# Exponentials and value products of two attentions run four and seven beats ahead of their maxima, with rewritten joints to the feed-forward stages

## The chip, the core and the metric

The kernel runs on one core of a Trainium2 chip. The metric is the device time of one execution in microseconds (us); the time before is the median of three runs. The engines are TensorE (PE), VectorE (DVE), ScalarE (ACT), GpSimd (POOL) and SyncE (SP), which only issues DMAs here. Each engine executes its own instructions strictly in order and waits on semaphores.

## What is computed

For 16 sequences of 512 tokens and 128 features, in float32, four sublayers follow each other, each added to its input:

```python
x = x + attn_a(layernorm(x))   # 16 heads of 8, causal mask, three heads up-weight a token region
x = x + ffn(layernorm(x))      # silu(x w1) * (x w2), gelu(h1), gelu(h2), w3; hidden width 512
x = x + attn_b(layernorm(x))   # 16 heads of 8, rotary q and k, no mask
x = x + ffn(layernorm(x))      # the same weights
# attention: softmax(q k^T / sqrt(8)) v, heads concatenated, output projection
```

## The kernel before

**Stages.** The first attention ("causal") goes over all 16 sequences, then the first feed-forward stage (FFN) over all 16, then the second attention ("rotary"), then the second FFN. A sequence is called a batch below. A function `attention` makes the code of both attentions, `feed_forward` that of both FFN stages. At a joint, the end of one stage and the start of the next are written into each other by hand.

**An attention is a pipeline of steps, and a step is a row of beats.** A step has 20 beats (causal) or 32 (rotary). In step n five batches are in work: x of batch n+1 is normalised, transposed and projected to q; k and v of batch n are made; the row maxima of batch n-1 are found; scores, exponentials and value products of batch n-2 are made; the result of batch n-3 is normalised and that of batch n-4 projected. One beat of the maxima is some matmuls into `ps_max` (L1003, L1020) and one reduction of VectorE (`negmax`, L854 or L850). One beat of the scores, for a pair of heads and 128 keys each, is matmuls into two of the three banks of `ps_score` (L985), two exponentials of ScalarE into `prob` (L971), and, causal, a mask on GpSimd that waits for both (L708). Value products (L1043) gather in `ps_out` over a group of beats; four times in a batch ScalarE copies `ps_out` to `o_raw` (`group_out`, L934), at score beats 8, 13, 18 and 23 (causal) or 12, 20, 28 and 36 (rotary). A score beat of 20 (32) and over lies in the next step.

**The order** is set by two tables, `CAUSAL_AT` and `ROTARY_AT`, that give each piece of work its beat in each engine's loop, and by the order in which a step's beat is written. For every engine the program is one list made by the loops `tensor`, `vector`, `scalar`, `pool_step`. On PE a beat is the scores, the maxima, the value products, then other work (`order`: S, M, W, X).

**The maxima go into the scores** as two more rows of the stationary q ("aug"). GpSimd splits the negated maxima in two bf16 parts (`P_nm0`, `P_nm1`, for the first and second half of the heads), PE transposes them (`nm0`, `nm1`), ScalarE copies them to `nm_rows` (`A_nm0`, `A_nm1`, L908), and SP sends them into `stack_q` by DMA (L548). The scores of the first half of the heads wait for the first of these, the scores of the second half (score beat 10 or 16) for the second.

**The queue of SP** in step n is, in this order: load of `stack_q` of batch n (L592), which waits until the parts stored last have landed; load of x of batch n+3 (causal, L282); second aug of batch n-2; `den` and four `o_num` out of `o_raw` of batch n-3 (L555, L558); store of the parts of k of batch n (L580, six DMAs); store of the reciprocals (L563); load of `stack_k` (L592); four `o_rden` (L570); first aug of batch n-1; store of the parts of q of batch n+1 (L580, six DMAs). Steps 8 and 9 of the causal attention have one more small DMA each, for a flag that says whether FFN weights have a low part (`FLAG_STEP`, L629).

**`o_raw` is one buffer.** The first copy of a batch waits until all four `o_num` of the batch ahead of it have landed:

```python
def group_out(act, b, G):
    act.wait_ge(s["pv"], count(BLOCKS, b, BLOCKS // GROUPS * (G + 1)))
    wait(act, s["den"], count(16, b))
    wait(act, s["o_in"], count(64, b))
    act.activation(m["o_raw"][:, G], m["ps_out"][:], ACT.Copy).then_inc(s["o_raw"], 1)
```

**q and k** come to DRAM in three bf16 parts, which GpSimd makes in two pieces: `high` (L671, L673; rotary, also the sum L668, after VectorE's `turned`, L831) at beats `P_q1`, `P_k1`, and `middle_low` (L678, L680) at `P_q2`, `P_k2`. In the causal attention these stand between masks: at beat 16 `high` of q, then the mask of beat 16, at beat 17 `middle_low` of q. The normalisation (L313 to L322) is at beat 7, ahead of the mask of that beat, and `middle_low` of k at beat 8.

**At a joint** PE finishes the step without maxima (B + 1), reads the flag, branches (`tensor_both`, two versions of the FFN code), and then mixes the last value products with the first FFN products. In the last batch of the first FFN the first maxima of the rotary attention are mixed in.

## Time and profile before

| | us |
|---|---|
| median of 3 runs | 2166.25 |
| lowest and highest | 2159.3, 2166.3 |
| the profiled execution | 2165.54 |
| its span | 2163.4 |
| PE busy | 1941.8 (90%) |
| VectorE busy | 1724.5 (80%) |
| ScalarE busy | 1475.7 (68%) |
| GpSimd busy | 1092.3 (50%) |

The stages lie one after another in the span: causal attention to about 613 us, FFN to about 955, rotary attention to about 1780, FFN to the end. A share over the whole span says little for one of them; the sections below read single steps (a causal one is 406.90 to 440.10, a rotary one 1394.30 to 1440.60). "Idle before" in a row is time in which the engine did nothing ahead of the instruction, with the instruction or DMA that ended it.

### The profile page before, as it was taken

The page shows a single profiled execution, that of the slowest core. Times are in us where ns is not written, and L with a number is a line of the kernel's source. Part 1 is how long each engine was busy: PE and PEld are TensorE (multiplying, and loading weights), DVE is VectorE, ACT ScalarE, POOL GpSimd, SP SyncE. Part 2 cuts the span into 40 slices and gives each one's busy share as a digit, 9 for nine tenths or more (in the row PEclk, how much of TensorE's full clock was granted, in tenths as well). Part 3 has the DMA queues.
Part 4 walks back from the last instruction along what each step waited for, and adds up shares of the span by engine and source line. Part 5 has one row for each costly group of instructions (what it writes and reads, how often), then busy time and mean ns, then how long its engine had stood idle before and what let it go on. Part 6 is the DMA issues. An engine that isn't in the chain of part 4 may idle for free.

```text
span 2163.4 us, 43052 instructions
## 1 busy us (share of the span) xinstructions
PE 1941.8 (90%) x16196; PEld 987.2 (46%) x16196; DVE 1724.5 (80%) x2353; ACT 1475.7 (68%) x2633; POOL 1092.3 (50%) x1550
## 2 busy tenths in 40 slices
PE   3888987998869999986799999999999978999998
PEld 1333443433337777764222222222222226777776
DVE  4888886887758888865899898999989926888883
ACT  1477776776856666642488888888888874666665
POOL 5777776776535555555333333434333013555554
PEclk6799998999989999998799999999999988999999
DMA  7456655655200000003444443344445000000000
GB/s 174 94 116 131 118 110 113 133 114 114 39 18 29 1 1 1 1 1 71 77 81 90 87 91 71 71 91 90 97 77 100 18 13 12 15 11 15 10 15 15
DMA packets 106357, 136.71 MB, mean 63 GB/s; under 512 B 21153, under 2 KB 90018, under 8 KB 100002
## 3 DMA queue, kind: packets, MB, share of 16 engines
q1 hardware_dynamic: 106146, 133.89, 30.8%
q8 instruction: 133, 2.18, 0.4%
q14 instruction: 78, 0.64, 0.1%
HBM read 67.78 MB, written 55.58 MB: 57 GB/s over the span
## 4 chain that ended last, share of the span: by engine, by line
PE 52%; POOL 11%; SPq 10%; DMA 10%; issue 8%; DVE 6%; ACT 4%; POOLq 0%; ACTq 0%; DVEq 0%
PE ps_score L1416 21%; PE ps_out L1043 8%; PE ps_max L1416 6%; PE ps_score L985 5%; DMA o_num<-o_raw 4%; PE ps_max L1003 4%; DVE negmax L854 4%; SPq L580 3%; DMA d_stack<-parts 3%; PE ps_out L1416 2%; ACT prob L971 2%; PE ps_max L1084 2%; SPq L558 2%; POOL xhat L322 2%; DMA stack_q<-nm_rows 2%
## 5 line engine op out<-in xcount | busy, mean ns | idle before, releaser
L971 ACT ACTIVATE prob<-ps_score 128x512 f32<-128x512 f32 x1664 | 898.9, 597 | 191.7 <-PE ps_score L985 173.6
L854 DVE TENSOR_REDUCE negmax<-ps_max 128x2 f32<-128x1024 f32 (+1 forms) x896 | 907.5, 1064 | 144.0 <-PE ps_max L1020 88.6
L1043 PE MATMUL ps_out<-prob,v_aug 128*9 128x256 f32 (+2 forms) x6656 | 514.4, 389 | 24.7 <-ACT o_raw L934 22.0
L1416 PE MATMUL ps_score<-h,w_hi 128*128 128x512 f32 x2048 | 506.3, 401 | 0.7 <-ACT h2f L1333 0.4
L1416 PEld LDWEIGHTS ps_score<-h,w_hi 128*128 128x128 f32 x2048 | 387.0, 191 | 96.4 <-issue 3.7
L985 PE MATMUL ps_score<-stack_q,stack_k 50*128 50x512 bf16 (+3 forms) x2048 | 358.1, 349 | 59.6 <-ACT prob L971 46.4
L1003 PE MATMUL ps_max<-stack_k,stack_q 48*128 48x512 bf16 (+3 forms) x2048 | 343.5, 353 | 59.8 <-DVE negmax L854 28.7
L1195 POOL TENSOR_TENSOR h<-h3f,h 128x512 fp32r<-128x512 f32 x128 | 191.5, 1506 | 159.9 <-ACT h L1339 159.9
L708 POOL TENSOR_SCALAR_AFFINE_SELECT prob<-prob 128x256 f32<-128x256 f32 (+1 forms) x448 | 188.3, 440 | 148.7 <-ACT prob L971 148.1
L985 PEld LDWEIGHTS ps_score<-stack_q,stack_k 50*128 50x128 bf16 x2048 | 105.5, 94 | 312.6 <-ACT prob L971 241.1
L1043 PEld LDWEIGHTS ps_out<-prob,v_aug 128*9 128x9 f32 x6656 | 106.2, 89 | 300.7 <-ACT prob L971 147.2
L1195 POOL TENSOR_TENSOR h<-h2f,h 128x512 fp32r<-128x512 f32 x128 | 173.4, 1356 | 63.3 <-ACT h L1339 63.3
L1003 PEld LDWEIGHTS ps_max<-stack_k,stack_q 48*128 48x128 bf16 x2048 | 87.5, 95 | 218.4 <-DVE negmax L854 99.5
L1333 ACT ACTIVATE h3f<-ps_score,s_col 128x512 f32<-128x512 f32 x128 | 87.6, 684 | 144.1 <-PE ps_score L1416 133.1
L668 POOL TENSOR_TENSOR qf<-qf,turned 128x512 f32<-128x512 f32 x32 | 41.2, 1286 | 262.3 <-DVE turned L831 262.3
L1416 PE MATMUL ps_max<-ffn_xT,w_hi 128*128 128x512 f32 x512 | 147.4, 422 | 20.4 <-DVE ffn_xT L1257 10.7
L1250 DVE CAST h<-h1f 128x512 fp32r<-128x512 f32 x128 | 130.5, 1020 | 38.5 <-PE ps_score L1416 34.6
L1333 ACT ACTIVATE h2f<-ps_score,s_col 128x512 f32<-128x512 f32 x128 | 88.1, 688 | 88.9 <-PE ps_score L1416 86.2
L1237 DVE SCALAR_TENSOR_TENSOR ut<-tanh,ps_max 128x512 f32<-128x512 f32 x128 | 86.9, 679 | 59.4 <-ACT tanh L1345 56.6
L332 DVE TENSOR_SCALAR xhat<-x,mv,rstd 128x128 f32<-128x128 f32 x128 | 94.5, 797 | 44.1 <-POOL rstd L304 44.1
L1252 DVE TENSOR_TENSOR h<-h1f,h 128x512 fp32r<-128x512 f32 x128 | 118.8, 928 | 4.4
L1416 PEld LDWEIGHTS ps_max<-ffn_xT,w_hi 128*128 128x128 f32 x512 | 95.6, 197 | 54.3 <-DVE ffn_xT L1257 23.7
(107 smaller groups left out, 2105.2 us busy)
## 6 DMA issues: line engine op xcount, KB each, us to landing
d_stack<-parts SPq DMA_DIRECT2D x128, 192.0 KB, 2.8
stack_q<-d_stack SPq DMA_DIRECT2D x64, 384.0 KB, 5.6
stack_k<-d_stack SPq DMA_DIRECT2D x64, 384.0 KB, 6.1
d_stack<-parts SPq DMA_DIRECT2D x128, 128.0 KB, 2.8
d_stack<-parts SPq DMA_DIRECT2D x128, 64.0 KB, 2.5
o_num<-o_raw SPq DMA_DIRECT2D x128, 64.0 KB
o_rden<-d_rden SPq DMA_DIRECT2D x128, 64.0 KB
x<-in_x SPq DMA_DIRECT2D x16, 256.0 KB, 6.9
```

The costliest lines, as they stand in the source:

```text
L332: last = dve.tensor_scalar(m["xhat"][:, t, :], m["x"][:, b % B, t, :], m["mv"][:, t, 0:1], m["rstd"][:, t:t + 1], ALU.subtract, ALU.mult)
L708: last = pool.affine_select(out=tri, in_=tri, compare_op=ALU.is_ge, fill=0.0, base=0, pattern=[[0, tri.shape[1]], [1, P]], channel_multipl ...
L854: last = dve.tensor_reduce(m["negmax"][:, t, :, p], banks[:, :, at:at + w], AX.X, ALU.max, negate=True)
L971: act.activation(prob(b, i)[:, o], act_bank("score", 2 * i + o), ACT.Exp).then_inc(s["prob"], 1)
L985: mm = pe.matmul(act_bank("score", 2 * i + o)[:, at:at + w], m["stack_k"][c][rows, p, P * j:P * (j + 1)], m["stack_q"][c][rows, p, S - w:S ...
L1003: last = pe.matmul(to[:, o, at:at + w], m["stack_q"][c][rows, p, P * t:P * (t + 1)], m["stack_k"][c][rows, p, 0:w], start=(piece == 0), st ...
L1043: last = pe.matmul(m["ps_out"][32 * g:32 * g + HD + 1, out:out + w], m["v_aug"][b % VALUES][:, j, 4 * G + g, :], prob(b, beat)[:, g % 2, l ...
L1195: pool.tensor_tensor(h[k][:, 1, f], hf[k][:, f % 2], h[k][:, 0, f], ALU.subtract).then_inc(s[f"h{k}"], 1)
L1250: dve.tensor_copy(h[1][:, 0, f], h1f[:, f % 2]).then_inc(s["h1_hi"], 1)
L1252: dve.tensor_tensor(h[1][:, 1, f], h1f[:, f % 2], h[1][:, 0, f], ALU.subtract).then_inc(s["h1"], 1)
L1333: act.activation(hf[k][:, f % 2], m["ps_hid"][:, f % 2], ACT.Gelu, scale=m["s_col"][:, k, f:f + 1]).then_inc(s[f"h{k}f"], 1)
L1416: mm = pe.matmul(to, w[:, cols], moving(part), start=begin and i == 0, stop=last and i == len(pairs) - 1)
```

## The change

**Shift.** Both tables get a number `ahead`: 4 beats (causal) and 7 (rotary). In beat i of step n, PE makes the scores and value products, ScalarE the exponentials and the copies to `o_raw`, and GpSimd the masks, of position i + ahead; positions past the end belong to the next step. Maxima, q, k, v, normalisation, aug copies and the whole queue of SP stay at their beats, but for the entries of the tables that the diff shows. So the first copy to `o_raw` of batch n-2 stands at beat 4 of step n (causal; it was 8) and at beat 5 (rotary; it was 12), and the first scores of batch n-1 at beat 16 (of 20) and beat 25 (of 32) of step n, not at beat 0 of step n+1.

**Tables.** Causal: `nm0` and `A_nm0` one beat earlier; the second piece of low weights at beat 8 of step 1, not 13. Rotary: `nm0` 23 to 18, `P_nm0` 19 to 16, `A_nm0` 24 to 19, `P_nm1` 8 to 0, `P_norm` 15 to 17, `xT`, `q` and their followers one beat later.

**Flag.** Its two DMAs go from steps 8 and 9 to 10 and 11, the reduction that reads it from step 10 to 13.

**Joints.** PE takes the branch four beats ahead of the end of the scores, and the first FFN gate follows at the end of the scores. In an FFN's first batch ScalarE makes the high part of h1 and GpSimd the low part; VectorE made both. At the end of the first FFN fewer of the first rotary maxima stand between its last products (2, 2 and 2 beats before, 3, 2 and 2 now), and VectorE, not GpSimd, makes the parts of the first k.

```diff
-W_LOW_AT = ((0, 19), (1, 13), (1, 5), (1, 5), (1, 5))
+W_LOW_AT = ((0, 19), (1, 8), (1, 5), (1, 5), (1, 5))
...
-CAUSAL_AT = {... "nm0": 13, ... "A_nm0": 14, ... "order": "MSWX"}
-ROTARY_AT = {... "xT": 19, "nm0": 23, "q": 23, ... "P_nm1": 8, "P_norm": 15,
-             "P_q1": 24, ... "P_nm0": 19, ... "D_q": 24, ... "A_nm0": 24, "A_xT": 20, "order": "SMWX"}
+CAUSAL_AT = {... "nm0": 12, ... "A_nm0": 13, ... "order": "MSWX", "ahead": 4}
+ROTARY_AT = {... "xT": 20, "nm0": 18, "q": 24, ... "P_nm1": 0, "P_norm": 17,
+             "P_q1": 25, ... "P_nm0": 16, ... "D_q": 25, ... "A_nm0": 19, "A_xT": 21, "order": "SMWX", "ahead": 7}
...
+    def ahead(n, i):
+        return divmod(BEATS * n + i + AHEAD, BEATS)
...
-        if causal and n == FLAG_STEP:
+        if causal and n == FLAG_STEP + 2:
...
-            if causal and on(n, 2):
-                mask(pool, n - 2, i)
+            step, at = ahead(n, i)
+            if causal and on(step, 2):
+                mask(pool, step - 2, at)
...
-            for lag, G in plan.out_due(i):
-                if on(n, lag):
-                    group_out(act, n - lag, G)
+            step, k = ahead(n, i)
+            for lag, G in plan.out_due(k):
+                if on(step, lag):
+                    group_out(act, step - lag, G)
...
+            step, k = ahead(n, i)
             for part in AT["order"]:
-                if part == "S" and on(n, 2):
-                    scores(pe, n, i)
+                if part == "S" and on(step, 2):
+                    scores(pe, n, step - 2, k)
...
-        gates(first, 0)
-        gates(first, 1)
-        before.tensor(pe, B + 2)
-        gates(first, 2)
-        gates(first, 3)
-        pe.wait_ge(over["prob"], count(2 * before.plan.beats, B))
-        transposes(pe, first + 1)
+        gates(first, 0)
+        before.tensor(pe, B + 1, scored)
+        gates(first, 1)
+        pe.wait_ge(over["prob"], count(2 * before.plan.beats, B))
+        transposes(pe, first + 1)
+        gates(first, 2)
+        gates(first, 3)
```

**ScalarE, causal, a steady step.** `nm_rows` ahead of `prob x2` or `x4` and `o_raw` is the second aug copy. Before:

```order
105 L908 ACTIVATE nm_rows<-ps_score 16x512
106 L971 ACTIVATE prob<-ps_score 128x512 x2
107 L934 ACTIVATE o_raw<-ps_out 128x512
108 L971 ACTIVATE prob<-ps_score 128x512 x6
109 L925 ACTIVATE v_aug<-ps_max 128x64x8
110 L971 ACTIVATE prob<-ps_score 128x512 x4
111 L934 ACTIVATE o_raw<-ps_out 128x512
```

Now:

```order
107 L933 ACTIVATE nm_rows<-ps_score 16x512
108 L996 ACTIVATE prob<-ps_score 128x512 x4
109 L959 ACTIVATE o_raw<-ps_out 128x512
110 L996 ACTIVATE prob<-ps_score 128x512 x4
111 L950 ACTIVATE v_aug<-ps_max 128x64x8
```

The `o_raw` of row 107 before is the batch's last copy; the first copy of the next batch is row 111, twelve exponentials and a value copy behind the aug copy. Now the first copy is row 109, four exponentials behind the aug copy.

**ScalarE, rotary, a steady step**, from the second aug copy to the batch's first copy to `o_raw`. Before:

```order
640 L908 ACTIVATE nm_rows<-ps_score 16x512
641 L934 ACTIVATE o_raw<-ps_out 128x512
642 L971 ACTIVATE prob<-ps_score 128x512 x16
643 L934 ACTIVATE o_raw<-ps_out 128x512
644 L971 ACTIVATE prob<-ps_score 128x512 x8
```

Now:

```order
634 L933 ACTIVATE nm_rows<-ps_score 16x512
635 L996 ACTIVATE prob<-ps_score 128x512 x2
636 L959 ACTIVATE o_raw<-ps_out 128x512
637 L996 ACTIVATE prob<-ps_score 128x512 x16
638 L959 ACTIVATE o_raw<-ps_out 128x512
```

Sixteen exponentials stood between the two; now two do.

**GpSimd, causal, around the parts of q** (beats 15 to 17), before:

```order
223 L708 AFFINE_SELECT prob<-prob 128x4x128
224 L708 AFFINE_SELECT prob<-prob 128x2x128
225 L671 CAST parts<-qf 128x512
226 L673 TENSOR_TENSOR rest<-qf,parts 128x512
227 L708 AFFINE_SELECT prob<-prob 128x2x128
228 L678 CAST parts<-rest 128x512
229 L680 TENSOR_TENSOR parts<-rest,parts 128x512
```

Now:

```order
218 L714 AFFINE_SELECT prob<-prob 128x2x128 x6
219 L714 AFFINE_SELECT prob<-prob 128x4x128
220 L677 CAST parts<-qf 128x512
221 L679 TENSOR_TENSOR rest<-qf,parts 128x512
222 L714 AFFINE_SELECT prob<-prob 128x2x128
223 L684 CAST parts<-rest 128x512
224 L686 TENSOR_TENSOR parts<-rest,parts 128x512
```

The mask ahead of the parts of q was that of score beat 15 and is that of score beat 19, the last of a batch; the one between their halves was that of score beat 16 and is the first of the next batch.

## Rows read from the trace of the kernel before

**Rows 1.** The page: busy time, share and instructions of each engine.

```profile
PE 1941.8 (90%) x16196; PEld 987.2 (46%) x16196; DVE 1724.5 (80%) x2353; ACT 1475.7 (68%) x2633; POOL 1092.3 (50%) x1550
```

**Rows 2.** By stretch: length, busy PE, PEld, DVE, ACT, POOL; PEclk, DMA, GB/s.

```profile
406.90:440.10 33.20, 30.55 (x400) 13.06 (x394) 27.88 (x42) 25.15 (x49) 25.45 (x52) 0.95 0.61 121
...
1394.30:1440.60 46.30, 43.21 (x422) 12.32 (x421) 41.80 (x47) 38.46 (x72) 16.29 (x24) 1.00 0.42 83
```

**Rows 3.** Waits of the whole span: who waited for whom, us, times, longest.

```profile
ACT o_raw L934 <- DMA o_num<-o_raw: 44.6, 22, 11.4
```

**Rows 4.** Timeline of ScalarE, one causal step: start, us, operation, count, idle before.

```profile
433.52 0.60 ACT L934 ACTIVATE o_raw<-ps_out 128x512 f32<-128x512 f32 x1 [2.65 <-DMA o_num<-o_raw]
...
437.37 1.08 ACT L971 ACTIVATE prob<-ps_score 128x512 f32<-128x512 f32 x2 [0.55 <-PE ps_score L985]
...
444.42 3.44 ACT L971 ACTIVATE prob<-ps_score 128x512 f32<-128x512 f32 x6 [0.44 <-PE ps_score L985]
...
449.64 2.14 ACT L971 ACTIVATE prob<-ps_score 128x512 f32<-128x512 f32 x4
```

**Rows 5.** Timeline of GpSimd, the same step.

```profile
430.01 0.24 POOL L313 TENSOR_SCALAR var<-mv 128x4 f32<-128x4 f32 x1
...
433.77 0.78 POOL L708 TENSOR_SCALAR_AFFINE_SELECT prob<-prob 128x256 f32<-128x256 f32 x2
...
435.20 1.16 POOL L680 TENSOR_TENSOR parts<-rest,parts 128x512 bf16<-128x512 f32 x1
...
447.13 0.61 POOL L671 CAST parts<-qf 128x512 bf16<-128x512 f32 x1
```

**Rows 6.** Timeline of SP's queue, the same step and the next.

```profile
443.88 2.78 SPq L570 DMA_DIRECT2D o_rden<-d_rden  x4
446.70 1.39 SPq L548 DMA_DIRECT2D stack_q<-nm_rows  x2
451.18 3.90 SPq L580 DMA_DIRECT2D d_stack<-parts  x6
...
458.54 1.37 SPq L548 DMA_DIRECT2D stack_q<-nm_rows  x2
```

**Rows 7.** Chain of work that ended last: start, us, what; landings of DMAs.

```profile
381.45 3.78 DMA stack_q<-nm_rows
...
454.46 2.42 DMA d_stack<-parts
...
462.86 4.25 DMA o_num<-o_raw
```

**Rows 8.** Timeline of VectorE: reciprocals, causal steps 3 and 15, rotary 3 and 15.

```profile
130.45 0.54 DVE L862 RECIPROCAL rden<-den 128x64 f32<-128x64 f32 x1
...
541.19 0.54 DVE L862 RECIPROCAL rden<-den 128x64 f32<-128x64 f32 x1
...
1120.07 0.54 DVE L862 RECIPROCAL rden<-den 128x64 f32<-128x64 f32 x1
...
1669.26 0.54 DVE L862 RECIPROCAL rden<-den 128x64 f32<-128x64 f32 x1
```

**Rows 9.** Timelines of one rotary step: VectorE, then ScalarE.

```profile
1414.38 0.75 DVE L831 SCALAR_TENSOR_TENSOR turned<-ps_max,bias_col,rope 128x512 f32<-128x512 f32 x1 [0.22 <-PE ps_max L1084]
...
1425.47 3.31 ACT L971 ACTIVATE prob<-ps_score 128x512 f32<-128x512 f32 x6 [0.36 <-PE ps_score L985]
1429.84 5.53 ACT L971 ACTIVATE prob<-ps_score 128x512 f32<-128x512 f32 x10 [1.06 <-PE ps_score L985]
1436.56 0.60 ACT L934 ACTIVATE o_raw<-ps_out 128x512 f32<-128x512 f32 x1 [1.19 <-DMA o_num<-o_raw]
```

**Rows 10.** Chain of work, around the flag's DMA in step 8.

```profile
311.19 11.17 DMA d_stack<-parts
```

**Rows 11.** Timelines of PE at the first joint and the rotary attention's last step.

```profile
616.83 3.75 PE L1416 MATMUL ps_max<-ffn_xT,w_hi 128*128 128x512 f32 x8 [3.98 <-issue]
...
1742.30 0.59 PE L1054 MATMUL ps_score<-ident_b,nm_parts 128*16 128x128 bf16 x4 [4.24 <-POOL nm_parts L653]
```

More of the change, by code:

```diff
@@ L440, in attention @@
     for i in range(BEATS):
-        act_turns += [("score", 2, 2 * i + o) for o in range(2)]
+        step, at = ahead(0, i)
+        act_turns += [("score", 2 - step, 2 * at + o) for o in range(2)]
         dve_turns += [("max", 1, i)]
@@ L900, in vector @@
             gate_scales(dve)
-        if causal and hi == BEATS and n == FLAG_STEP + 2:
+        if causal and hi == BEATS and n == FLAG_STEP + 5:
             flag_of_weights(dve)
@@ L946, in scalar @@
             weights_hi(act)
-        if causal and n == 2 and lo == 0:
-            act.wait_ge(s["w_lo"], len(W_PIECES))
         for i in range(lo, hi):
+            if causal and ahead(n, i) == (2, 0):
+                act.wait_ge(s["w_lo"], len(W_PIECES))
             if i == AT["A_nm1"] and on(n, 2):
@@ L1204, in pool_layer @@
         left["weighted"](pool, B - 2)
+        for f in range(FT):
+            pool.wait_ge(s["h1_hi"], count(FT, first, f + 1))
+            pool.tensor_tensor(h[1][:, 1, f], h1f[:, f % 2], h[1][:, 0, f], ALU.subtract).then_inc(s["h1"], 1)
+        left["weighted"](pool, B - 1)
         for r in range(B):
@@ L1222, in pool_layer @@
                 fill["high"](pool, 0, "q", 0)
-                low(pool, b, 3, range(0, 2))
                 fill["middle_low"](pool, 0, 0)
-                low(pool, b, 3, range(2, 4))
-                fill["high"](pool, 0, "k", 1)
-                fill["middle_low"](pool, 0, 1)
+                low(pool, b, 3, range(FT))
             if r == B - 1:
@@ L1277, in vector_layer @@
         norm_apply(dve, m, s, first + 1)
-        for r in range(-1, B - 1):
+        gated(dve, first, 0)
+        gated(dve, first, 1)
+        for f in (2, 3):
+            dve.wait_ge(s["h1"], count(FT, first, f - 1))
+            gated(dve, first, f)
+            if f == 2:
+                left["invert"](dve, B - 1)
+        xT_low(dve, first + 1)
+        left["residual"](dve, B - 2)
+        for r in range(B - 1):
             b = first + r
+            fill = after.parts if after is not None and r == B - 2 else None
             gated(dve, b + 1, 0)
             gated(dve, b + 1, 1)
-            if after is not None and r == B - 2:
-                after.parts["project"](dve, 0, "q", 0)
-                after.parts["turn"](dve, 0, "q", 0)
-            if r == -1:
-                dve.wait_ge(before.s["pv"], count(before.plan.blocks, B))
-            if 0 <= r < B - 2:
+            if r < B - 2:
                 normed(b + 2)
+            if fill:
+                fill["project"](dve, 0, "q", 0)
+                fill["turn"](dve, 0, "q", 0)
             split(dve, b + 1, 0)
+            if fill:
+                fill["project"](dve, 0, "k", 1)
             split(dve, b + 1, 1)
-            if r == -1:
-                left["invert"](dve, B - 1)
-                left["residual"](dve, B - 2)
             if r == 0:
                 left["residual"](dve, B - 1)
-            if r > 0:
+            else:
                 add_y(dve, b - 1)
@@ L1299, in vector_layer @@
             split(dve, b + 1, 2)
-            if after is not None and r == B - 2:
-                after.parts["project"](dve, 0, "k", 1)
-                after.parts["turn"](dve, 0, "k", 1)
+            if fill:
+                fill["turn"](dve, 0, "k", 1)
+                fill["parts_on_vector"](dve, 0, "k", 1)
             gated(dve, b + 1, 3)
@@ L1308, in vector_layer @@
                 after.parts["statistics"](dve, 0)
-            if after is not None and r == B - 2:
-                after.parts["whole_bias"](dve, m["ps_misc"][:, 0:D])
-                after.parts["statistics"](dve, 1)
+            if fill:
+                fill["whole_bias"](dve, m["ps_misc"][:, 0:D])
+                fill["statistics"](dve, 1)
         add_y(dve, first + B - 2)
@@ L1360, in scalar_layer @@
         xT_high(act, first)
-        before.scalar(act, B + 1, 12)
+        scored = before.plan.beats - before.plan.at["ahead"]
+        before.scalar(act, B + 1, 12, scored)
         gate(act, first, 0)
+        before.scalar(act, B + 1, scored)
         gate(act, first, 1)
-        before.scalar(act, B + 2)
-        for r in range(-1, B):
+        high(act, first, 0)
+        high(act, first, 1)
+        gate(act, first, 2)
+        high(act, first, 2)
+        gate(act, first, 3)
+        xT_high(act, first + 1)
+        high(act, first, 3)
+        for r in range(B):
             b = first + r
@@ L1435, in layer @@
                         mm.then_inc(s[f"l{k}_ps"], 1)
-                if between is not None and i == 1:
-                    between()
         def gates(n, f):
@@ L1463, in tensor_layer @@
             layer(b, 2, (0,))
+            if r == 0:
+                gates(b + 1, 0)
+                gates(b + 1, 1)
             if fill and r == B - 2:
@@ L1539, in tensor_both @@
         transposes(pe, first)
-        before.tensor(pe, B + 1, 10)
+        before.tensor(pe, B + 1, 10, before.plan.beats - before.plan.at["ahead"] - 4)
         pe.wait_ge(s["halved"], 5)
```

116 lines of the change are left out of this document (65 added, 51 removed).

## The prediction, made blind

> **What bounds the kernel now.** The busy shares come first, and they mislead: PE is 90% busy and VectorE 80% [rows 1], so a schedule that packs beats more tightly looks like the thing to want. The stretches by step say more. A causal step takes 33.2 us with 30.55 of PE and 25.15 of ScalarE, a rotary step 46.3 with 43.2 of PE and 41.8 of VectorE [rows 2]: close to the engines' work, but not at it. What ends last in a step stands in the waits. The batch's first copy to `o_raw` waits for the `o_num` DMAs of the batch ahead, 22 times and 44.6 us in all [rows 3]. In the causal step read here it waited 2.65 us [rows 4], in the rotary one 1.19 [rows 9]. So in both attentions the copy is where a loop through ScalarE, GpSimd, SP's queue and two DMAs closes, and it has no slack left.
>
> The causal loop, from the copy at 433.52 to the next at 467.2: ScalarE runs score beats 8 to 15 until about 446.7 (four of six exponentials of the row that starts at 444.42) [rows 4]; GpSimd masks and starts the parts of q at 447.13 [rows 5]; SP stores them from 451.18 [rows 6]; they land at 456.88 (454.46 + 2.42) [rows 7]; SP loads `stack_q`, sends the second aug at 458.54 [rows 6], then `den` and `o_num`; the last `o_num` is issued at 462.86 and lands at 467.11 [rows 7]. That is 13.2 us on ScalarE, 0.4 for mask and start, 20.0 from the parts to the landing: 33.6. The twelve steps from the reciprocal at 130.45 to that at 541.19 [rows 8] took 34.2 each, or 33.4 without ten us lost near the flag (below).
>
> **The shift, causal.** The exponentials and copies move four beats ahead; SP's queue and the parts of q do not. The copy now stands at beat 4 and waits for the same DMAs, still issued behind the parts of q of beat 17. ScalarE has beats 4 to 15, score beats 8 to 19, between the copy and the mask ahead of the parts. Score beats 16 to 19 end at 451.8 (449.64 + 2.14) [rows 4], 5.1 us behind beat 15. So this loop alone gives 13.2 + 5.1 + 0.4 + 20.0 = 38.7.
>
> A second wait enters it. The mask between the halves of the parts of q is now the first of the next batch, whose scores need the first aug at beat 16. That aug is late in SP's queue. Counted from the copy (0): score beat 10 ends at 4.9 (437.37 + 1.08 - 433.52) [rows 4]; one mask 0.4; the normalisation 3.8 (430.01 to the mask at 433.77); two masks 0.8; the second half of the parts of k 1.9 (masks' end near 434.5 to 436.36) [rows 5]: 11.8. SP then stores k, 3.9 like q; landing 2.4 from the last issue: 17.5. Load of `stack_k` 0.8, `o_rden` 2.8, aug 1.4 [rows 6]: last issue at 21.8. It lands 3.8 to 3.9 later [rows 7]: 25.7, where ScalarE could have had beat 16 at 18.3. Scores and two exponentials 1.4, mask 0.4, second half of q 1.9: 29.4. From the store of q to the landing of `o_num` is 467.11 - 451.18 = 15.9. The period is **45.3 us** and not 33.4: +11.9. Over twelve steps, with the flag's ten us kept in either, that is +143. The steps of the last two batches have no q to store, but keep the wait from second aug to `o_num` (from 458.54 to 467.11, 8.6 us, against four exponentials, 2.2) and a shorter one at beat 16: about 7 + 7 + 4.5 + 7 less 5 of waits that were there, +20. At the start, -5 for four beats that are overlapped, +11 for the same two waits: +6. Causal sum **+169**.
>
> **The shift, rotary.** No masks here, and the first aug has ten beats from the reciprocal (beat 15) to beat 25, 14 us at 1.43 a beat. Behind the reciprocal come its store with a landing (3.3, estimated from the 0.6 and 2.4 of other stores), `o_rden` 2.8, the aug 0.7 to its last issue and 3.8 to land [rows 6, 7]: 10.6. I give it nothing. The loop runs from the copy to `turned` of beat 28, then parts, store, load, second aug, `o_num`, copy. From the end of `turned` at 1415.13 to the idle's end at 1436.5 is 21.4 [rows 9], none of which moves. The copy goes from beat 12 to beat 5; in between ScalarE now has 9.9 us (1425.47 to 1435.37) [rows 9]. The twelve steps from 1120.07 to 1669.26 [rows 8] took 45.8 each, so the loop becomes 45.8 + 9.9 = 55.7 at most; PE and VectorE may lose some gaps, of which they have 3 to 4.5 in a step [rows 2]: I take **55**, +9.2, or +110 over twelve. A check that does without q: the second aug copy stands two exponentials (1.1 us) ahead of the copy to `o_raw`, and aug, `den`, `o_num` and landing take 8.6 (458.54 to 467.11) [rows 6, 7], so ScalarE stands for 7.5 a step whatever else happens, and 45.8 - 1.2 + 7.5 is 52. The last two steps have this wait alone, +16. At the start +8 for the first such wait and -6 for seven overlapped beats: +2. Rotary sum **+128**.
>
> **The gains.** A beat of scores alone is 1.1 us (two exponentials) [rows 4] and one of maxima alone I estimate at 1.2, both together 33.4/20 = 1.67 or 45.8/32 = 1.43; four and seven fewer of each alone are worth about 3 and 6, counted above. `P_nm1` at beat 0 puts the split of the last maxima ahead of the FFN's normalisation on GpSimd: PE's wait of 4.24 us goes [rows 11], with some slow matmuls behind it: -5.5. The branch ahead of the last four beats of scores: the 3.98 us of issue at the joint [rows 11] can lie behind queued exponentials, and the mixed order saves some more. I take -8 at each joint (bounds 0 and -12), -16. High parts on ScalarE for one batch, fewer maxima between the last FFN products, the earlier second piece of low weights: each touches a single batch, 0 within 3 us either way. Sum of gains **-21.5**.
>
> **The flag.** In step 8 the store of q landed 11.17 us after its last issue instead of 2.4 [rows 10], with the flag's DMA issued right behind it. It is the only landing of that length in the chain, and the only store with that DMA behind it; the pair is kept two steps later, so I take 0. If the delay was its step's, -9.
>
> **Sum.** 2165.5 (the profiled execution, 0.7 below the median) + 169 + 128 - 21.5 = 2441; I say **2440 us**, 12.6% slower. About 0.5%, 11 us, is what a measurement here tells from no change.
>
> **Rivals.**
> 1. *The copy's wait alone.* If in the causal attention the first aug is in time (parts of k earlier on GpSimd than I count, or a quicker queue), its loop is 38.7: 12 x 6.6 and some 10 at the ends less, **2350**. For it: the queue has gaps that I fill. Against: the sum of issues alone, from the parts of k to the aug, is 3.9 + 0.8 + 2.8 + 1.4 us with two landings, and the reciprocal at beat 12 gates it too. Chance 0.2.
> 2. *The work packs around the wait.* The floor is PE's work plus a stand of 7 us: causal about 36, rotary about 51, so 12 x 2.6 + 12 x 5.2 + 44 (the ends, as above) - 21.5, **2280**. PE would have to run nearly without gaps outside the wait. Chance 0.06.
> 3. *Faster.* The waits cost nothing, because `o_num` lands before ScalarE gets to the copy. The price is then -3 - 6 - 21.5: **2135**. It decides at the point where the second aug and `o_num` take less than the two to four exponentials between: 8.6 us against 1.1 and 2.2. The 2.65 and 1.19 us of idle at today's places speak against it. Chance 0.03.
> 4. *The clock.* After today's wait PE runs slowly for a while: the causal step has a mean clock of 0.95, the rotary 1.00 [rows 2]. Two long stands a step (causal) and one (rotary) would leave more of the work at 1.2 GHz: 0.05 of 33 us is 1.7 us a time, over 24 steps some +40, **2480**. Chance 0.1. The Trainium skill states this in "TensorE: Matmul & The Clock Gate", Part 1: a PE that idles long enough is gated to half rate and speeds up only once busy again. It speaks against the change, which lengthens idling; today's rotary wait of 1.19 us with a clock of 1.00 shows the other side of it. By that rule the sum would be this rival's, by the rotary row my forecast's.
> My forecast, 2400 to 2470, has 0.6; 0.01 is left for within 0.5% of before.
>
> **How the numbers follow.** The range goes from rival 1's 2350 to rival 4's 2480; rivals 2 and 3, the 0.01 and the far side of either end are left out, 0.1 and some 0.08. Faster by over 0.5% 0.03, within 0.5% 0.01, slower 0.96.
>
> **What would show it.** The wait of `o_raw` on `o_num` in some 26 places, 5 to 10 us each, in place of 44.6 us in all. Reciprocals 45 us apart (causal) and 55 (rotary). In the causal attention a wait of the first scores of a batch on `stack_q<-nm_rows`, 5 to 8 us; if it is under 1 us, rival 1. The 4.24 us wait gone. FFN steps unchanged near 21.7. A store of q that lands ten us late near the flag's new step, or not. Wrong in kind would be a wait at the copy below 3 us in the steady steps.

## The result

The changed kernel took **2512.3 us** (median of four runs, 2510.9 to 2515.9) against 2165.0 before (2159.3 to 2166.3), a ratio of 1.161 (95% interval 1.159 to 1.164): 16% slower. The forecast was 2440, range 2350 to 2480. Direction and mechanism came as told. The size did not: 72 us are missing, and the time lies 32 above the range. The profiled execution took 2515.9 us, with a span of 2514.2 and a mean granted clock of 0.886 (before: 2163.4 and 0.950).

The page of the changed kernel has the same 16196 matmuls as [rows 1], but they are busy 74 us longer. Its PEclk line gives TensorE's granted clock in 40 slices, in tenths of full speed:

```profile
PE 2015.9 (80%) x16196; PEld 997.6 (40%) x16196; DVE 1725.4 (69%) x2342; ACT 1480.1 (59%) x2641; POOL 1099.9 (44%) x1553
...
PEclk6778788878888899999698888899898889999999
```

The waits (us in all, times, longest). The first answers to [rows 3]; the other two, weight loads and matmuls of the same scores, overlap:

```profile
ACT o_raw L959 <- DMA o_num<-o_raw: 238.8, 30, 14.6
...
PEld ps_score L1010 <- DMA stack_q<-nm_rows: 112.5, 18, 10.7
PE ps_score L1010 <- DMA stack_q<-nm_rows: 108.9, 18, 9.1
```

The reciprocals of causal steps 3 and 15 and rotary steps 3 and 15, as in [rows 8]:

```profile
148.25 0.54 DVE L887 RECIPROCAL rden<-den 128x64 f32<-128x64 f32 x1
...
739.34 0.54 DVE L887 RECIPROCAL rden<-den 128x64 f32<-128x64 f32 x1
...
1338.83 0.54 DVE L887 RECIPROCAL rden<-den 128x64 f32<-128x64 f32 x1
...
2024.79 0.54 DVE L887 RECIPROCAL rden<-den 128x64 f32<-128x64 f32 x1
```

A causal step takes 49.3 us instead of 34.2, a rotary one 57.2 instead of 45.8. Over twelve steps each that is +180 and +137, together 317 of the 347.

**One causal step**, from the first copy to `o_raw` of one batch to that of the next. ScalarE (start, us, operation, idle before):

```profile
577.67 0.60 ACT L959 ACTIVATE o_raw<-ps_out 128x512 f32<-128x512 f32 x1 [6.08 <-DMA o_num<-o_raw]
...
582.43 0.60 ACT L950 ACTIVATE v_aug<-ps_max 128x512 f32<-128x512 f32 x1 [2.04 <-PE ps_max L1112]
...
606.82 1.09 ACT L996 ACTIVATE prob<-ps_score 128x512 f32<-128x512 f32 x2 [7.78 <-PE ps_score L1010]
...
625.92 0.60 ACT L959 ACTIVATE o_raw<-ps_out 128x512 f32<-128x512 f32 x1 [6.04 <-DMA o_num<-o_raw]
```

SP's queue in the same step, which stands as in [rows 6]:

```profile
591.23 3.89 SPq L586 DMA_DIRECT2D d_stack<-parts  x6
...
597.46 0.79 SPq L598 DMA_DIRECT2D stack_k<-d_stack  x2
598.29 2.78 SPq L576 DMA_DIRECT2D o_rden<-d_rden  x4
601.11 1.39 SPq L554 DMA_DIRECT2D stack_q<-nm_rows  x2
610.21 3.91 SPq L586 DMA_DIRECT2D d_stack<-parts  x6
...
617.32 1.37 SPq L554 DMA_DIRECT2D stack_q<-nm_rows  x2
...
619.45 3.20 SPq L564 DMA_DIRECT2D o_num<-o_raw  x4
```

And the landings, from the chain of work that ended last (start, us):

```profile
509.55 10.22 DMA d_stack<-parts
...
594.52 2.88 DMA d_stack<-parts
...
601.84 4.24 DMA stack_q<-nm_rows
...
621.65 4.17 DMA o_num<-o_raw
```

Read them in turn. Parts of k are stored from 591.23. Their landing lets `stack_k` be loaded, then come `o_rden` and the first aug, whose last issue at 601.84 lands at 606.08. Only then do TensorE's scores and ScalarE's exponential at 606.82 go on, after a stand of 7.78 us. The parts of q, held up behind that score beat's mask on GpSimd, are stored from 610.21, and behind them stand the load, the second aug and `o_num`, which lands at 625.82. The copy at 625.92 waited 6.04 us for it. Both waits that the forecast named are there, and both are in one loop of 48.3 us (the first row of this list, 509.55, belongs to the flag, below).

**TensorE's rate behind a stand** is what the sum did not price. By stretch of one rotary step (length, busy time of PE, PEld, DVE, ACT, POOL, then the clock): the stand for the copy, then the seven us behind it.

```profile
1773.00:1782.00 9.00, 0.59 (x5) 0.09 (x4) 1.97 (x2) 0.48 (x2) 0.00 (x0) 0.62 0.66 122
1782.00:1789.00 7.00, 6.41 (x34) 1.15 (x34) 2.39 (x3) 3.39 (x7) 0.55 (x1) 0.51 0.00 0
```

A clock of 0.51 is the lower of the two levels, 1.2 GHz instead of 2.4. The products of this stretch show it in their length, 2.08 us for a pair of the same line that takes 1.12 at 1770.79, ahead of the stand:

```profile
1785.51 2.08 PE L1109 MATMUL ps_max<-xT,weights 128*128 128x512 f32 x2
```

The clock fell in this way in every one of the twelve rotary steps; its mean over them is 0.90.

### The profile page after: what moved, and what is told of

It is laid out like the page before. It is cut to its first block, busy times and chain, and to the rows that moved or that the text cites. A ratio compares the mean times of both kernels' runs of the same rounds, so it can differ in the third digit from the quotient of the medians.

```text
span 2514.2 us, 43055 instructions
## 1 busy us (share of the span) xinstructions
PE 2015.9 (80%) x16196; PEld 997.6 (40%) x16196; DVE 1725.4 (69%) x2342; ACT 1480.1 (59%) x2641; POOL 1099.9 (44%) x1553
## 4 chain that ended last, share of the span: by engine, by line
PE 52%; SPq 12%; DMA 12%; issue 8%; POOL 8%; ACT 5%; DVE 3%; POOLq 0%; ACTq 0%; DVEq 0%
PE ps_score L1460 18%; PE ps_out L1068 10%; PE ps_score L1010 7%; DMA o_num<-o_raw 5%; PE ps_max L1460 5%; PE ps_max L1028 4%; SPq L586 4%; ACT prob L996 4%; DMA d_stack<-parts 3%; DMA stack_q<-nm_rows 3%; SPq L564 2%; PE ps_max L1109 2%; PE ps_out L1460 2%; SPq L554 2%; SPq L576 2%
## 5 line engine op out<-in xcount | busy, mean ns | idle before, releaser
L1068 PE MATMUL ps_out<-prob,v_aug 128*9 128x256 f32 (+2 forms) x6656 | 549.0, 412 | 158.7 <-ACT o_raw L959 152.8
L1010 PE MATMUL ps_score<-stack_q,stack_k 50*128 50x512 bf16 (+3 forms) x2048 | 380.0, 367 | 234.6 <-ACT prob L996 118.6
L1460 PEld LDWEIGHTS ps_score<-h,w_hi 128*128 128x128 f32 x2048 | 381.9, 188 | 104.6 <-POOL h L1233 10.8
L1028 PE MATMUL ps_max<-stack_k,stack_q 48*128 48x512 bf16 (+3 forms) x2048 | 356.5, 364 | 45.1 <-DVE negmax L879 24.1
L674 POOL TENSOR_TENSOR qf<-qf,turned 128x512 f32<-128x512 f32 x31 | 39.5, 1274 | 469.3 <-DVE turned L856 469.3
L959 ACT ACTIVATE o_raw<-ps_out 128x512 f32<-128x512 f32 x128 | 77.1, 602 | 243.3 <-DMA o_num<-o_raw 238.8
L875 DVE TENSOR_REDUCE negmax<-ps_max 128x4 f32<-128x1024 f32 x64 | 77.4, 1209 | 119.4 <-PE ps_max L1045 118.7
L1275 DVE CAST h<-h1f 128x512 fp32r<-128x512 f32 x120 | 124.4, 1037 | 34.8 <-PE ps_score L1460 33.7
```

Of the source, the lines that this page charges most:

```text
L1010: mm = pe.matmul(act_bank("score", 2 * i + o)[:, at:at + w], m["stack_k"][c][rows, p, P * j:P * (j + 1)], m["stack_q"][c][rows, p, S - w:S ...
L1028: last = pe.matmul(to[:, o, at:at + w], m["stack_q"][c][rows, p, P * t:P * (t + 1)], m["stack_k"][c][rows, p, 0:w], start=(piece == 0), st ...
L1068: last = pe.matmul(m["ps_out"][32 * g:32 * g + HD + 1, out:out + w], m["v_aug"][b % VALUES][:, j, 4 * G + g, :], prob(b, beat)[:, g % 2, l ...
L1275: dve.tensor_copy(h[1][:, 0, f], h1f[:, f % 2]).then_inc(s["h1_hi"], 1)
L1460: mm = pe.matmul(to, w[:, cols], moving(part), start=begin and i == 0, stop=last and i == len(pairs) - 1)
```

## The experiments

"Spacing" is always the mean distance of twelve reciprocals, taken as in [rows 8], causal and rotary. All kernels are edits of the changed one unless it says otherwise.

| kernel | us | causal | rotary | wait of `o_raw`, all |
|---|---|---|---|---|
| before | 2165.0 | 34.2 | 45.8 | 44.6 |
| changed | 2512.3 | 49.3 | 57.2 | 238.8 |
| without shift | 2134.5 | 34.0 | 45.8 | 50.3 |
| causal shift alone | 2341.0 | 48.6 | 45.7 | 110.6 |
| rotary shift alone | 2300.3 | 34.4 | 56.9 | 158.4 |
| half the shift | 2305.2 | 40.7 | 51.1 | 77.2 |
| numerators first | 2421.8 | 46.5 | 53.2 | 141.5 |
| first aug first | 2418.5 | 42.6 | 57.3 | 267.4 |
| both | 2305.5 | 38.5 | 53.0 | 146.5 |
| both, second aug too | 2292.7 | 37.9 | 53.0 | 144.4 |
| no shift, numerators first | 2106.6 | 33.3 | 44.7 | 0.8 |
| no shift, both | 2104.8 | 33.2 | 44.7 | 3.5 |
| before, numerators first | 2152.1 | 34.4 | 45.2 | 3.2 |

### The parts of the change

**No shift.** The tables, the flag's place and the joints stay new; both shifts are zero.

```diff
-CAUSAL_AT = {... "order": "MSWX", "ahead": 4}
-ROTARY_AT = {... "order": "SMWX", "ahead": 7}
+CAUSAL_AT = {... "order": "MSWX", "ahead": 0}
+ROTARY_AT = {... "order": "SMWX", "ahead": 0}
...
+        if not before.plan.at["ahead"]:
+            before.tensor(pe, B + 2)
```

ScalarE's list gets the same two lines.

> The changed kernel with both shifts set to 0 (scores, exponentials, copies and masks back at their beats); the changed joints, the other table entries and the later flag stay. Theory (the shift alone costs, through the copy to o_raw that waits for the o_num DMAs): within -30 to 0 us of the kernel before, 2135 to 2165, causal reciprocals 33 to 34 us apart, rotary ones 45 to 46. Rival (the other table entries or the joints carry part of the loss): above 2200. If the flag's small DMA is the cause of the ten us in step 8, they appear in step 10 or 11 instead.

Measured: 2134.5 us, a ratio of 0.988 (0.985 to 0.991) to before, and the spacing is that of before. So all else in the change is worth -27 us (forecast -21.5), and the shift alone costs 378. The -27 is against the 2161.7 that the kernel before took beside this one; against the 2165.0 of the table it is -30.5.

The flag's write (L635) stands right behind the store of q here too, but the ten us did not come with it. The store's last issue is at 381.45 and `stack_q`, which waits for its landing, is loaded from 383.57, so it landed within 2.1 us:

```profile
377.54 4.52 SPq L586 DMA_DIRECT2D d_stack<-parts  x6
382.10 0.58 SPq L635 DMA_DIRECT2D d_flags<-flags  x1
383.57 3.60 SPq L598 DMA_DIRECT2D stack_q<-d_stack  x2
```

**Each shift alone**, one of the two numbers set to zero (and the joint's lines as above).

> The changed kernel with the rotary shift set to 0, the causal shift of 4 kept. Theory: the causal steps stay 49 apart and the rotary ones go back to 46, so 2512 less 12 x 11.3 and the two waits at the end of the rotary attention (16) = 2360, within 15. Rival (the two shifts share one cost, such as one of the joints): the saving is under 80 us.

> The changed kernel with the causal shift set to 0, the rotary shift of 7 kept. Theory: the causal steps go back to 33.5, the rotary ones stay at 57: 2512 less 12 x 15.1 (49.3 - 34.2) and some 25 at the ends = 2305, within 15. e2 and e3 together minus e1 should give the changed kernel within 10 us.

Measured: 2341.0 (causal) and 2300.3 (rotary), 4 us under the band of the first and inside that of the second. Against the kernel without shift the causal one costs 207 us, the rotary one 166. Their sum on 2134.5 is 2507, 5 below the changed kernel, so the two hardly act on each other.

**Half the shift**, two beats and three.

```diff
-CAUSAL_AT = {... "order": "MSWX", "ahead": 4}
-ROTARY_AT = {... "order": "SMWX", "ahead": 7}
+CAUSAL_AT = {... "order": "MSWX", "ahead": 2}
+ROTARY_AT = {... "order": "SMWX", "ahead": 3}
```

> The changed kernel with half the shift: two beats in the causal attention, three in the rotary one (the joints then finish what is left over). Theory: each beat of shift puts its own length between the copy to o_raw and the transfers that it waits for, so the loop grows in proportion: rotary about 50.5 us (45.8 unshifted, 57.2 with seven), causal about 42 (34.0 and 48.6 to 49.3), some 2310 us in all, 2270 to 2340. Rival: the schedule has slack for a few beats and the waits set in only beyond them: 2200 us or less.

Measured: 2305.2 us. The rotary step grows by 5.3 us for three beats and 11.4 for seven, 1.8 and 1.6 a beat; the causal one by 6.7 for two and 15.3 for four, 3.4 and 3.8 a beat. There is no sign of a threshold: the price starts with the first beats, as it must in a loop that had no slack.

### The order in SP's queue

**Numerators first.** `den` and `o_num` stand ahead of the load of `stack_q` and the second aug. They need the last copy to `o_raw` and, because `o_num` is one buffer too, the product `oT` of the batch ahead (GpSimd, beat 1 causal, 0 rotary), but not the parts of q.

```diff
+        if on(n, 3):
+            numerators(sp, n - 3)
         if on(n, 0):
             load(sp, n, "stack_q", "stored_q", 0)
         if causal and on(n, -X_AHEAD):
             load_x(sp, m, a, n + X_AHEAD)
         if on(n, 2):
             aug(sp, 1, n - 2)
-        if on(n, 3):
-            numerators(sp, n - 3)
```

> The changed kernel with one move in SP's queue: den and o_num stand ahead of the load of stack_q and of the second aug. Theory (the copy to o_raw waits for o_num behind the parts of q and the second aug): o_num then waits for the store of q and for oT of GpSimd's beat 1 (causal) or 0 (rotary); it lands about 1.5 us earlier in the causal step and 4 in the rotary one, so 2512 - 12 x 1.3 - 12 x 4 = 2450, within 20, and the copy's wait of 8.5 us in a rotary step falls to 4 or 5. Rival (the wait at the copy is not what sets the period, but PE work at the half clock or the first aug): less than 15 us.

Measured: 2421.8 us, 91 less, more than the band allowed. The copy's wait falls from 238.8 to 141.5 us, as the theory has it, while the wait for the first aug stays:

```profile
ACT o_raw L959 <- DMA o_num<-o_raw: 141.5, 30, 5.9
...
PEld ps_score L1010 <- DMA stack_q<-nm_rows: 106.1, 27, 10.5
```

The numerators are then held up in part by `oT` (SP waits 52.3 us for it, in 16 places).

**First aug first.**

```diff
+        if on(n, 1):
+            aug(sp, 0, n - 1)
         if on(n, 3):
             store_reciprocals(sp, n - 3)
         if on(n, 0):
             load(sp, n, "stack_k", "stored_k", 1)
         if on(n, 3):
             spread_reciprocals(sp, n - 3)
-        if on(n, 1):
-            aug(sp, 0, n - 1)
```

> The changed kernel with one issue moved in SP's row: the first augmented row of batch n-1 stands ahead of the store of the reciprocals and the load of parts of k, instead of behind them. Theory: at the causal part's block boundary TensorE's next score tile (beat 16) waits for that transfer; issued at the end of the beat before it lands some 6 us earlier, so this wait all but ends, while the wait of the first o_raw copy, which comes from the second half of the row, stays. The causal step falls from 49.3 us to about 43 us, the rotary one stays at 57.2: about 2440 us. Rival: the wait for the first row only covers time that the copy wait would take anyway (the loop closes over the second half); then under 20 us is won.

Measured: 2418.5 us, 94 less, 22 below the 2440 expected. The causal step is 42.6, the rotary one unchanged at 57.3. The wait for the first aug is gone and the copy's has grown, the other way round than in the run before:

```profile
ACT o_raw L959 <- DMA o_num<-o_raw: 267.4, 30, 14.4
...
PEld ps_score L1010 <- DMA stack_q<-nm_rows: 5.7, 2, 4.5
```

The two runs tell the two waits apart. The second wait is real, and it is worth 6.7 us a causal step. The forecast had 6.6 for it, the distance from rival 1's 38.7 to 45.3.

**Both, and the second aug ahead of the load of `stack_q` as well.**

```diff
+        if on(n, 3):
+            numerators(sp, n - 3)
+        if on(n, 2):
+            aug(sp, 1, n - 2)
         if on(n, 0):
             load(sp, n, "stack_q", "stored_q", 0)
```

> The changed kernel, fully shifted, with both moves in SP's row: the numerators ahead of the load of stack_q and the second augmented row, and the first augmented row ahead of the reciprocals' store. Theory: they cut two different waits, won about 90 and 94 us apart, so together 2330 us (2305 to 2350), still far above the unshifted kernel, since the parts of q stay unshifted ahead of both. Rival: one loop closes over both, and the second move gives nothing more: 2400 us or above.

> As the last one, with the second augmented row moved ahead of the load of stack_q too: now nothing stands ahead of numerators and augmented rows in SP's row but the store of the parts of q. Theory: the second row lands about 1 us earlier, in both attentions, 10 to 30 us below the last kernel. Rival: the load of stack_q is then late for the maxima and their first beats: no gain or a loss.

Measured: 2305.5 with both moves, 207 less than the changed kernel, where the two single gains add up to 184; 25 us below the point expected, at the band's edge. 2292.7 with the third move, 13 less, 7 of them in the causal steps. With nothing but the store of the parts of q ahead of them in the queue, the numerators still land late, 144.4 us in 30 waits, and the kernel is 158 us slower than the one without shift. No order of these transfers that I tried saves the shift while the parts of q stay at their beat. The numerators ahead of the store of q, or the parts of q moved with the exponentials, were not tried.

### The missing 72 us: the clock behind the stands

The waits were as foreseen, so the suspect was the stretch at half clock. To price it, TensorE gets work in its stand that enters nothing of the result: matmuls into the next maxima bank, which is written anew before it is read.

```diff
+    def keep_busy(pe, n, i, products):
+        dve_banks_free(pe, n, "max", i)
+        for _ in range(products):
+            pe.matmul(dve_banks("max", i)[:, 0, 0:S], ...)
...
                     if part == "W" and on(step, lag):
+                        if rotary and block == BLOCKS // GROUPS and 3 <= n < B:
+                            keep_busy(pe, n, i + 1, ...)
                         weigh(pe, step - lag, block)
```

**First try**: 32 bf16 matmuls of 512 columns with the operands of the maxima. They have 48 rows (`48*128` in the trace), not the 50 that the expectation of the second try names.

> The changed kernel with work added that computes nothing of the result: in each rotary step 3 to 15, where TensorE stands for the first o_raw copy, 32 matmuls of 512 columns run into a max bank that is overwritten later. Theory: what the forecast's sum lacked is the stretch at half clock behind this stand; with the engine busy in it the clock stays up, the rotary step falls from 57.2 us to 54.5 to 55, and the kernel to about 2480 us although it does some 90 us more of TensorE work. Rival: the long step is the transfers' chain alone and the half clock lies beside it: under 8 us of change, or slower by what the added work hangs over.

Measured: 2517.0 us, rotary spacing 57.5: nothing gained. But nothing was tested either, since the clock fell during the added work. The same columns as above, first 4.6 us of it, then the rest and what follows:

```profile
1713.20:1717.80 4.60, 4.57 (x22) 2.01 (x23) 1.11 (x1) 0.00 (x0) 0.00 (x0) 1.00 0.89 153
1717.80:1728.20 10.40, 10.30 (x38) 2.38 (x36) 1.89 (x2) 2.73 (x6) 0.00 (x0) 0.51 0.16 25
```

**Second try**: 14 float32 products over all 128 rows.

> The changed kernel with work added that computes nothing of the result, in the stand of each rotary step 3 to 15: 14 float32 matmuls of 512 columns over all 128 rows of the array, instead of 32 bfloat16 ones over 50 rows, which did not keep the clock up. Theory: what counts for the clock is how much of the array works, then the half clock behind the stand goes and the rotary step falls from 57.2 us to about 55, some 30 us in all (2480). Rival: no such work changes the clock in this stretch: within 8 us of 2512.

Measured: 2520.1 us, rotary spacing 57.9. The clock stayed up this time, in the stand and behind it:

```profile
1661.30:1673.60 12.30, 12.24 (x32) 5.27 (x36) 1.13 (x1) 1.57 (x3) 0.00 (x0) 1.00 0.44 81
1673.60:1680.00 6.40, 6.40 (x63) 1.51 (x62) 4.85 (x5) 4.29 (x8) 2.65 (x3) 1.00 0.00 0
```

By its number this is the rival's (within 8 us of 2512), but not by its reason, since the clock did change. The work is 12.3 us long and the stand about 9, so some 3 us hang over, as much as the clock can give back. The third try tests that.

**Third try**: 10 such products, 8.9 us.

> As the last one with added float32 work over 128 rows, but 10 products (20 passes, about 8.8 us) instead of 14 (12.3 us), so that the work ends with the stand of 9 us. Nothing of it enters the result. Theory: the half clock behind the stand costs about 2.3 us a step, which the forecast lacked: rotary step 57.2 to 54.5 to 55.2, kernel 2480 to 2490 us. Rival: the stretch at half clock lies beside a longer chain and costs nothing: rotary step 57 and more, 2510 or above.

Measured: **2480.0 us**, 32 less, with more work done. The stand and the stretch behind it, then the reciprocals of rotary steps 3 and 15:

```profile
1699.90:1708.80 8.90, 8.85 (x24) 3.76 (x28) 1.13 (x1) 0.69 (x2) 0.00 (x0) 1.00 0.61 110
1708.80:1716.00 7.20, 7.20 (x73) 1.73 (x74) 5.66 (x6) 5.97 (x12) 3.46 (x4) 1.00 0.01 3
```

```profile
1339.85 0.54 DVE L887 RECIPROCAL rden<-den 128x64 f32<-128x64 f32 x1
...
1994.20 0.54 DVE L887 RECIPROCAL rden<-den 128x64 f32<-128x64 f32 x1
```

The seven us behind the stand now hold 73 matmuls, not 34. The step is 54.5 us, where the forecast had 55 and the changed kernel has 57.2. So the half clock costs 2.6 us a rotary step, 32 over twelve, the whole gain of this run. The granted clock of the twelve steps is 1.00, where it was 0.90, and the copy's wait is the same (234.1 us in all): the chain of transfers did not change.

**The same in both attentions**, with 7 products ahead of the scores of beat 0 and 5 ahead of those of beat 9 in the causal one.

```diff
+                if causal and part == "S" and k in (0, 9) and 3 <= n < B:
+                    keep_busy(pe, n, i + 1, {0: 7, 9: 5}[k])
```

> The same, and in the causal steps 3 to 15 too: 7 products (6.1 us) ahead of the scores of beat 0, where TensorE stands for the first augmented row, and 5 (4.4 us) ahead of those of beat 9, where it stands behind the o_raw copy. Nothing of it enters the result. Theory: the causal step falls from 49.3 to 46 or 47 us (the forecast had 45.3), kernel 2435 to 2460 us. Rival: in the causal loop the half clock costs nothing, or the work hangs over: 2480 or above.

Measured: 2463.2 us, 17 less again and 3 above the band. The causal step is 47.3, and the granted clock of twelve causal steps is 0.97, where it was 0.82. The same causal code stood between 48.6 and 49.3 in the six profiles that have it, so keeping the clock gives back 1.3 to 2.0 us a step there. Where the added work hangs over a stand, this is less than what the clock costs.

**Rows or type?** 40 bf16 matmuls over 128 rows (8.5 us) in the rotary stand.

> The changed kernel with 40 bfloat16 matmuls of 512 columns over 128 rows (8.5 us) in the rotary stand; nothing of it enters the result. Theory: the rows of the array that work are what counts; the clock stays up as with float32, and the rotary step is 54.5 to 55.5. Rival: it is the type (float32 in two passes); then the clock falls as with the 50-row bfloat16 work, step 57.

Measured: 2490.5 us (two runs), rotary spacing 55.3, and the clock of the stand is 1.00:

```profile
1699.70:1708.30 8.60, 8.58 (x39) 3.72 (x38) 0.86 (x1) 0.00 (x0) 0.00 (x0) 1.00 0.73 128
```

So bf16 as such isn't what let the clock fall in the first try. The two bf16 kinds differ in their rows (48 and 128), and in their number (32 and 40) and length (6.8 us at full clock and 8.6).

### A version that beats both

The copy's wait is in the kernel before too [rows 3], and it needs no shift to be removed.

**No shift, numerators first**: the edits of those two kernels together.

> Both attentions unshifted (as in the run without shifts) and the new joints kept, with the transfers that put the numerators back (the reciprocal row and the product to o_num) issued ahead of the load of stack_q and the second augmented row in SP's queue. Theory: of the 1.9 us mean wait of the o_raw copy per step (50.3 us in 27) most ends, and TensorE's half clock behind it with it: causal step about 31.5 us instead of 34.0, rotary 44.8 instead of 45.8, so about 2095 us, 2070 to 2125. Rival: the load of stack_q, now behind the numerators, comes late for the next score tile and gives it back: within 15 us of 2134.

Measured: **2106.6 us**, 0.975 of before (0.971 to 0.979), 28 less than without the move; 12 above the point expected, inside its range; the causal step is 33.3 where 31.5 was expected. The wait at the copy is gone, while the weight loads of the scores now wait 25.0 us for aug rows, in 23 places (4.8 in 6 without the move):

```profile
ACT o_raw L959 <- DMA o_num<-o_raw: 0.8, 2, 0.6
```

The twelve rotary steps (1132.80 to 1667.60) have 519.67 of 534.80 us of PE busy, 97%, at a clock of 1.00, so little idle time is left in them.

**The first aug first as well.**

> As the unshifted kernel with the numerators issued first, and the first augmented row of batch n-1 issued first as well. Theory: in the unshifted loop TensorE waits little for that row, so the move gives 0 to 15 us over the kernel with the numerators first alone: 2080 to 2100 us. Rival: the reciprocals' store and the load of parts of k, now behind it, come later and lengthen the step: 2110 us or more.

Measured: 2104.8 us, 0.973 (0.969 to 0.978): 5 above the band expected and no different from the last within what can be measured. Without the shift the first aug has time.

**Before, numerators first**, the move alone in the kernel before.

> The kernel before with one move: the numerators ahead of the load of stack_q and the second augmented row in SP's row. Theory: the move is worth the same 28 to 30 us as in the unshifted version of the change, so 2130 to 2138 us, and the joints the rest. Rival: without the new joints the chain runs elsewhere: within 10 us of before.

Measured: 2152.1 us, 0.993 (0.991 to 0.995). The move gives some 14 us here and not the 28 to 30 expected; the rival, within 10, is nearer. The copy's wait falls from 44.6 to 3.2 us all the same, and the weight loads of the scores wait longer for aug rows (45.1 us in 33 places, 24.0 in 20 before). That wait grows by about 20 us with the move in the unshifted kernel too (4.8 to 25.0), where the move gives 28, so its growth doesn't tell the two apart. Why the move is worth only half here stays open.

## Why the prediction missed

The step that failed is the length of a steady step. The sum let TensorE do its work behind the stand at the full clock, and came to 55 us (rotary) and 46.1 (causal, with the flag's share). The runs showed 57.2 and 49.3, and 54.8 and 47.3 once TensorE's clock was kept up. That is 49 of the 72 us; the other 23 have no run that isolates them.

- **What bounds the kernel** held. The copy to `o_raw` closes a loop through SP's queue that had no slack. The half shift shows a price from the first beats on, and moving the numerators away, shift or not, shortens the wait.
- **The shift, rotary**: 166 us measured, 128 told. The steady step came out 57.2 and not 55, 26 us over twelve. Its transfers were nearly right: from the end of `turned` to the copy takes 20.4 us in the changed kernel (1761.58 to 1781.94), told 21.4. With the clock kept up the step is 54.5. The term that failed is "I take 55, from 55.7 at most": it let PE win back gaps after the stand, and gave no time to PE at half rate. The other 12 us are what is left for the start and end.
- **The shift, causal**: 207 measured, 169 told. The spacing is 49.3. Told were 45.3 a step and the flag's ten us, 46.1 on the mean of twelve; that is 3.1 us a step and 37 over twelve. The clock's share is 1.3 to 2.0 us a step. The step read above shows where such time enters: counted from the copy, the second half of the parts of k is done at 13.6 us (told 11.8), and ScalarE's value copy ahead of it waited 2.04 us for products at half rate (in that order; that the one caused the other was not tried); from there to the landing of the aug took 14.9 (told 13.9, with landings of 2.88 and 4.24 us where I had 2.4 and 3.8); scores, mask and second half of q took 4.1 (told 3.7); from the store of q to the landing of `o_num` 15.6 (told 15.9). Together 48.3, 3.0 more than told, as in the spacing. Some 1.3 to 2.0 us of it have been shown to be the clock's; the rest fits the later landings, which no run isolates. The wait for the first aug was sized well: in the run that takes it away the step is 42.6, as far above rival 1's 38.7 (39.5 with the flag's share) as 49.3 is above 46.1.
- **Rival 4** named the cause and was priced some 9 us too low. It took 5% of a causal step as the lower clock's cost, 1.7 us, and 40 us in all, and gave it a chance of 0.1 as something that might or might not come. But stands of this length were already in the forecast, and the clock fell behind them in every one of the twelve rotary steps. It should have been a term of the sum: 49 us have been measured by the run that keeps TensorE busy in both attentions, which leaves 2463, 23 above the forecast. Where the rule and the rotary row spoke against each other, I went by a row with an idle of 1.19 us and a clock of 1.00, and forecast stands of 7.5 us with it. The Trainium skill, "TensorE: Matmul & The Clock Gate", Part 1, says that an idle TensorE is gated to half rate and works itself back only when busy; the rows of the changed kernel agree (0.51 behind a stand of 9.0 us).
- **The gains**: -27 measured (the kernel without shift; -30.5 against 2165.0), -21.5 told. `P_nm1` did what was said: TensorE takes the split maxima of the last rotary step (2103.80) with no idle ahead, where [rows 11] had 4.24 us. The branch's stand at the first joint did not go. It is 3.37 us, against 3.98 before:

```profile
825.52 0.61 PE L1010 MATMUL ps_score<-stack_q,stack_k 50*128 50x512 bf16 x2 [3.37 <-issue]
...
2103.80 0.39 PE L1079 MATMUL ps_score<-ident_b,nm_parts 128*16 128x128 bf16 x4
```

- **The flag**: the 0 came out, but by luck. The store of q in front of its write, now in step 10, lands after 10.22 us (the row at 509.55 above; before 11.17 [rows 10]). The same pair stands in the kernel without shift, and there the store landed within 2.1 us. So the write behind it is not enough for the delay, and what causes it stays open. The interval around that step is longer all the same: 38.9 us there, where most are near 33.
- **Rivals 1 to 3** are out. The wait for the first aug is there in 18 places (rival 1), the steps are 13 and 6 us above the floors of rival 2 (its 36 and 51 are rough: PE's busy time in [rows 2] and a stand of 7 us make 37.6 and 50.2), and the copy waits for 30 of 32 batches (rival 3).

The sum as it stands now: 2165.0 - 30.5 + 206.5 + 166 is 2507, 5 below the measured time; 49 us of it go when TensorE's clock is kept up.

## What to carry over

Before shifting one part of a software pipeline against another, follow the buffer that both share around its whole loop, through the queue of the engine that issues the DMAs: if it has no slack, each beat of shift is paid in full (1.6 to 1.8 us a beat here in the rotary attention; 3.4 to 3.8 in the causal one, where a second wait enters), and reordering that queue alone can be worth more than the shift. When a forecast contains a stand of TensorE of several microseconds per step, put the half-rate work behind it into the sum as a term, not into the tail as a rival. A cheap test of that term is to fill the stand with matmuls that nobody reads, of the stand's length and no longer, and to look in the trace whether the clock stayed up before believing the result.

## What the hardware did that was not expected

- Keeping TensorE busy did not always keep its clock. With 32 bf16 matmuls of 512 columns over 48 rows, back to back, the granted clock fell from 1.00 to 0.51 after 4.6 us, in the midst of them. Behind 39 recorded ones over 128 rows, and 20 float32 passes over 128 rows, it stayed at 1.00. What of it the clock answers to, these runs don't settle.
- A store of 768 KB in six DMAs (the parts of q) landed 10.22 us after its last issue in the changed kernel and 11.17 in the one before, both times with the flag's write of 128 single values right behind it. The other landings of such stores on the two chains are 2.1 to 3.9 us. The same pair landed within 2.1 us in the kernel without shift, in 3.83 us in that with the causal shift alone, and in 3.98 in the third try above. The write is not enough to explain it; the cause stays open.
